# PV of two attention steps issued as one block on TensorE, in a fused attention and mixture-of-experts kernel on one core

## What is computed

```python
att = jnp.einsum('bhqd,bhkd->bhqk', q, k) / jnp.sqrt(jnp.float32(HS))
att = jnp.where(causal, att, jnp.float32(-1000000000.0))
att = jax.nn.softmax(att, axis=-1)
y = jnp.einsum('bhqk,bhkd->bhqd', att, v)
```

## Time and profile before

| | |
|---|---|
| median of three runs | 1422.44 us (1416.7 to 1422.6) |
| the profiled execution | 1421.05 us |
| its span | 1419.3 us, mean granted clock 0.94 |
| TensorE busy | 1271.5 us, 90% |
| VectorE busy | 1158.4 us, 82% |
| ScalarE busy | 777.7 us, 55% |
| GpSimd busy | 230.3 us, 16% |
| items read (line 680) | 768, 684 ns each |
| PV products (line 534) | 2560, 541 ns each |

### The profile page before, as it was taken

The page is one execution under the profiler, slowest core; times in us unless marked ns, Lnnn a source line. Parts: engine busy times, 40 slices in busy tenths (PEclk is TensorE's granted clock), DMA queues, the critical chain, the costliest instruction groups (busy, mean ns, idle before and its releaser), DMA issues. The chain is left out here.

```text
span 1419.3 us, 22655 instructions
## 1 busy us (share of the span) xinstructions
PE 1271.5 (90%) x7857; PEld 644.2 (45%) x7857; DVE 1158.4 (82%) x2780; ACT 777.7 (55%) x1098; POOL 230.3 (16%) x250
## 2 busy tenths in 40 slices
PE   8892997999999999999999999999578739999997
PEld 4550132333333333333333333332366539999997
DVE  6994997999999999899899999991276728888886
ACT  2441065666666666666666667668245435544442
POOL 1336000100100100101101100101234321111221
PEclk9995599999999999999999999999888859999999
DMA  6877496131131131121221210000545422343330
GB/s 206 255 240 167 62 155 146 31 90 32 31 91 31 33 88 32 48 74 31 61 60 32 75 46 10 23 2 16 165 142 181 154 92 93 101 142 117 96 105 21
DMA packets 120272, 126.91 MB, mean 89 GB/s; under 512 B 16604, under 2 KB 102751, under 8 KB 120160
## 3 DMA queue, kind: packets, MB, share of 16 engines
q1 hardware_dynamic: 116576, 117.01, 29.7%
q0 software_dynamic: 3584, 8.47, 1.7%
HBM read 83.02 MB, written 48.38 MB: 93 GB/s over the span
## 5 line engine op out<-in xcount | busy, mean ns | idle before, releaser
L625 ACT ACTIVATE probs<-scores 128x1024 f32<-128x1024 f32 (+3 forms) x640 | 539.0, 894 | 327.9 <-PE scores L518 327.0
L680 DVE TENSOR_REDUCE part_max<-ring 128x1 f32<-128x512 f32 x768 | 478.4, 684 | 24.0 <-PE ring L548 22.4
L548 PE MATMUL ring<-k_stack,q_stack 96*128 96x512 bf16 (+3 forms) x1280 | 407.1, 363 | 41.1 <-DMA k_stack<-pieces_d 26.2
L518 PE MATMUL scores<-q_stack,k_stack 99*128 99x512 bf16 (+3 forms) x1280 | 339.8, 350 | 9.9 <-DMA q_stack<-max_rows 7.6
L534 PE MATMUL out_p<-probs,v_s 128*32 128x512 f32 (+3 forms) x2560 | 300.2, 541 | 0.5 <-POOL probs L730 0.3
L548 PEld LDWEIGHTS ring<-k_stack,q_stack 96*128 96x128 bf16 x1280 | 114.9, 97 | 347.9 <-DVE part_max L680 148.7
L674 DVE CUSTOM_DVE_ANT_0 scratch<-ring,mask_s 128x384 f32<-128x384 f32 (+2 forms) x384 | 195.0, 551 | 18.0 <-issue 17.1
L730 POOL TENSOR_SCALAR_AFFINE_SELECT probs<-probs 128x512 f32<-128x512 f32 x128 | 81.6, 637 | 781.8 <-ACT probs L625 781.8
L518 PEld LDWEIGHTS scores<-q_stack,k_stack 99*128 99x128 bf16 x1280 | 113.0, 98 | 182.7 <-issue 64.3
L1394 PE MATMUL psY<-w_hi,h_hi 128*128 128x256 f32 x320 | 90.9, 284 | 0.0
L534 PEld LDWEIGHTS out_p<-probs,v_s 128*32 128x32 f32 x2560 | 50.6, 108 | 87.3 <-issue 56.2
(11 more groups left out here) (113 smaller groups left out, 1349.9 us busy)
## 6 DMA issues: line engine op xcount, KB each, us to landing
w_whole<-w SPq DMA_DIRECT2D x16, 1024.0 KB, 7.5
q_stack<-pieces_d SPq DMA_DIRECT2D x192, 64.0 KB, 3.0
k_stack<-pieces_d SPq DMA_DIRECT2D x192, 64.0 KB, 3.1
v_d<-vt SPq DMA_DIRECT2D x8, 1024.0 KB, 4.6
v_s<-v_d SPq DMA_DIRECT2D x8, 1024.0 KB, 6.0
o_d<-o_s SPq DMA_DIRECT2D x32, 256.0 KB, 2.2
p_o<-o_d SPq DMA_DIRECT2D x8, 1024.0 KB, 6.0
slots_d<-no_row SPq DMA_DIRECT2D x1, 5200.0 KB, 28.3
```

Source lines behind the costliest of these rows:

```text
L518: last = nc.tensor.matmul(scores[p][:, hh, off:CHUNK], k_stack[i][0:KROWS, kb // TPC, j, kb % TPC * P:(kb % TPC + 1) * P], q_stack[i][0:KR ...
L548: last = nc.tensor.matmul(slot[:, h * w:(h + 1) * w], q_stack[i][0:SROWS, qt // TPC, j + h, qt % TPC * P:(qt % TPC + 1) * P], k_stack[i][0 ...
L625: nc.scalar.activation(probs[n % NPROB][:, 2 * p:2 * p + 2, off:CHUNK], scores[p][:, :, off:CHUNK], ACT.Exp, scale=SCALE).then_inc(exp_don ...
L680: nc.vector.tensor_reduce(part_max[:, qt, j, t:t + 1], ring[m % 3][:, 0:w], axis=AX.X, op=ALU.max).then_inc(ring_read, 1)
```

## The change

PV is left out of the even steps, and an odd step n issues the PV of the steps n - 3 and n - 2 one directly after the other (`pv_pair`), in the place where it issued that of n - 2. Everything else on TensorE keeps its order, the items too. On ScalarE the copy of `out_p` after a chunk's last PV moves from behind the second exponential of an odd step to between the two exponentials of the even step after it. VectorE's, GpSimd's and SyncE's instructions stay as they are.

```diff
-assert NSTEP % NPROB == 0
+PAIR = 2
+assert NSTEP % NPROB == 0 and all(last % PAIR == PAIR - 1 for last in LAST)
...
                 items(u, i, uses, second, third, ahead)
                 if behind:
-                    pv_step(*behind)
+                    pv_pair(*behind)
                 items(u, i, uses, third, stop, ahead)
+
+            def pv_pair(u, i, n):
+
+                for m in range(n - PAIR + 1, n + 1):
+                    pv_step(u, i, m)
 
             def unit(u, i, uses, ahead):
 
                 for n in range(LAG, NSTEP):
                     if n == LAG:
                         pe.wait_ge(v_loaded[i], 16 * uses[0])
-                    step(u, i, uses, n, ahead, (u, i, n - LAG))
-                for n in range(NSTEP - LAG, NSTEP):
-                    if ahead:
-                        step(u + 1, 1 - i, uses[1:], n + LAG - NSTEP, ahead, (u, i, n))
-                    else:
-                        pv_step(u, i, n)
+                    step(u, i, uses, n, ahead, (u, i, n - LAG) if n % PAIR else None)
+                if ahead:
+                    for n in range(LAG):
+                        step(u + 1, 1 - i, uses[1:], n, ahead, (u, i, NSTEP + n - LAG) if n % PAIR else None)
+                else:
+                    pv_pair(u, i, NSTEP - 1)
...
             def exp_step(u, n):
                 off = STEPS[n][2]
                 for p in range(2):
+                    if p == 1:
+                        if n == LAG and u:
+                            copy_o(u - 1, 0)
+                        for c in ORDER:
+                            if n - LAG - 1 == LAST[c]:
+                                copy_o(u, c)
                     act.wait_ge(scores_ready[p], NSTEP * u + n + 1)
...
-            def unit(u, follows):
+            for u in range(UNITS):
                 for n in range(NSTEP):
                     exp_step(u, n)
-                    if n == LAG - 1 and follows:
-                        copy_o(u - 1, 0)
-                    for c in ORDER:
-                        if n - LAG == LAST[c]:
-                            copy_o(u, c)
-
-            unit(0, False)
-            for u in range(1, UNITS):
-                unit(u, True)
             copy_o(UNITS - 1, 0)
```

## The result

The changed kernel takes 1488.25 us (median of four runs, 1487.0 to 1489.9) against 1422.41 us for the kernel before (now four runs too), a ratio of 1.0464 with a 95% interval of 1.0442 to 1.0486: slower by 4.6%. The forecast was 1488.

A forecast was written before the change was run, and what follows sets the result against it. VectorE plus a small PV hole was taken to bound five-item steps, TensorE four-item ones. Seven units at 8.9 us (62), last unit 9.5, less 4 absorbed: +67 us on 1421, 1488 us, range 1455 to 1518.

The forecast's parts named there:

- The bound: Full-width attention steps with five items: VectorE bounds them, plus a 0.09 us hole from the PV block; 3.08 us per step.
- The hole: VectorE's standstill across a full-width joined PV block: 0.99 us in place of 0.09; eight cycles per unit lose 4.1 us.
- the 29 us faster: Rival: TensorE is the bound and saved switches shorten 160 pairs by about 0.2 us each, giving 1392 us; chance 0.05.
- The starts of chunks: Five cycles per unit at the start of a chunk or its maxima: the longer joined block adds 4.0 us.
- The narrow cycles: Seven cycles per unit with narrow blocks or four to five items: together +0.7 us, between -1 and +2.
- The 0.5 us for the copy in step 38: The moved copy of out_p lies between two exponentials of 256 columns and delays the next scores: +0.5 us.
- The last unit: Second-half scores wait for exponentials, some six cycles at about +1.0 us; with the first half's +3.5, +9.5 us.
- Unit 0: A TensorE wait for the DMA of a maximum's rows absorbs the 4 us lost before it.
- A sign that failed: In the list of waits, VectorE's idle before ring reads was to rise from 20.5 us to well over 100.
- The other signs: Unit 111 to 112 us, blocks 1.90, cycles 6.4 and 7.0, VectorE busy 95, TensorE waiting in its own row, clock 1.00.
- The rivals: Other outcomes: faster 0.05, cancelled out or not done 0.05, falling clock 0.04; those outside the range hold 0.14.
- The clock's: Rival: TensorE's pauses in the attention drop its clock to 1.2 GHz in one cycle of six, 117 us more, 1605; chance 0.04.

The follow-up runs named there:

- ring2_single: The kernel before with a ring of two PSUM banks in place of three: 1541.98 us, ratio 1.0847.
- ring4_single: The kernel before with a ring of four banks, one head's scores left out of the result: 1400.39 us, ratio 0.9843 to the kernel before.
- half_single: The kernel before with VectorE's plain ring reads cut from 512 to 256 columns: 1395.46 us, ratio 0.9822 to the kernel before.
- The ring experiments: The kernel before and the changed kernel, each rebuilt with two and four ring banks: 1541.98 and 1400.39 us, against 1606.45 and 1440.55.
- copy_back: The changed kernel with the copy of out_p put back behind the second exponential of an odd step: 1482.84 us, 1.0437 to the kernel before.
- half_joined: The changed kernel with VectorE's plain ring reads cut from 512 to 256 columns: 1436.11 us, ratio 1.0106 to the kernel before.
- ring2_joined: The changed kernel with a ring of two banks in place of three: 1606.45 us, ratio 1.1302 to the kernel before.
- split: The changed kernel with one item put between an odd step's two PV steps, where one is left: 1503.8 us, 1.0580 to the kernel before.
- ring4_joined: The changed kernel with a ring of four banks, one head's scores left out: 1440.55 us, ratio 1.0127 to the kernel before.

## Why the prediction was right

**The bound.** That the five-item step hangs on VectorE, with a hole of 0.09 us, was worked out from distances between rows, while the busy shares of TensorE and VectorE looked alike. `ring2_single` bears it out: the same sum with one read less gave its five-item step to 0.01 us. So do `ring4_single` and `half_single`: with the hole closed or the reads shorter, a full-width step of five items takes 3.05 us in both in place of 3.09. That is a small gain, and not where most of their 21 and 26 us come from, twice and more what was expected. In a mid-run unit of `ring4_single` (99.9 us for 102.8) most lies in steps with narrow scores or masked reads: step 12 falls from 3.09 to 2.84, since its five reads bound a step whose work on TensorE is less. In `half_single` 13 of the 26 us lie ahead of the first PV (173.7 us in place of 186.6), where the first maxima are made. So VectorE bounded the kernel before in more places than I had counted.

**The hole.** 0.99 us was forecast for a joined block and 0.94 measured, with a cycle of ten items at 6.83 us for 6.98 and of nine at 6.32 to 6.56 for 6.38 (6.45 where one item follows the block, 0.1 more, as it said). The block was 1.86 us, not 1.90: the second PV step pays neither start nor end, so it lies at the lower bound. The Trainium skill (TensorEngine Tiling (Array Packing), Key Properties) says that a change of the tiling mode, and not just of the tile, drains TensorE. The trace agrees: joining saved 0.14 us of two blocks' time and 0.10 of an entry. But the program did not get the 29 us faster that this alone was to give (160 pairs at 0.2 us would be 32), since TensorE's saved time fell into waits.

**The starts of chunks.** +4.0 us per unit as forecast. The working took the longer block to be paid in full there. The ring experiments show this for two of the five cycles (0.86 us with any number of banks); the other three cost less with two or four banks, so for them it is not shown.

**The narrow cycles** came out at +0.4 for +0.7. The 0.5 us for the copy in step 38 was right: by `copy_back` it is 0.46. Without the copy the joined order gains there, 2.99 us for 3.16, and the seven cycles together -0.1, where the working had left +0.2.

**The last unit** lost 10.6 us for 9.5. Its full-width joined cycles were right (5.03 for 5.07), but the same cycles before take 4.17 and not 3.94, so that they and four like them lose 0.86 each and not 1.0. On the other side I had put the two cycles whose even step is narrow at about nothing, and they lose 0.78 each: there, too, the scores of 128 columns wait for exponentials, now of 256.

**Unit 0.** I let 4 us be absorbed by the wait for a DMA. That wait shrank only from 7.6 to 5.8 us, so the absorption was 2. The mid-run units came out at +8.4 in place of +8.9 each (3 us less in all), the last unit and the clock at 1 and 2 us more, and the stages after the attention, which I had left alone, took 1.3 us less. These errors cancelled: forecast +67 us, measured +67.5 in the span. That the sum is right to a microsecond is luck to about the size of these terms, some 3 us.

**A sign that failed.** VectorE's idle time before plain reads of the ring was to rise from 20.5 us to well over 100. The list shows 57.9 (59 waits of about 1 us). VectorE's whole idle time from 250 to 970 us does come to 115, but only some nine waits in a unit stand before plain reads; the rest lies around the masked reads and at the starts of chunks. So this sign was put on the wrong row. The other signs came as written, the clock apart: unit, block, cycles, VectorE's busy time, and TensorE's waits for these reads in its own row (18.5 us, 0.6 before).

**The rivals.** The clock's was there, but small: 2 us where it would have been 117, since TensorE fell to 1.2 GHz in two places and not in every sixth cycle. The forecast's "1.00 throughout" was wrong by that much. The Trainium skill (TensorE: Matmul & The Clock Gate, A second HAM failure mode: psum-queue depth-cycling) tells of a kernel in which brief pauses between groups, as it goes round PSUM banks, make the clock swing. The traces agree in so far as in the joined order with two banks the clock fell twelve times. They don't say that the pauses do it: `ring2_single`, which waits too (TensorE busy 91% from 260 to 980 us, 93% in the changed kernel), has no such place. Why it fell where it did stays open; nothing was run for it.

## What to carry to other kernels

Where two engines hand each other buffers, look at the longest stretch in which the producer does something else, not at busy shares: the consumer lives through it only if (buffers + 1) times its time per buffer covers the stretch and the way through the ring (here 0.74 + 0.32 + 0.42 us, one read included). Joining work to save switches lengthens just that stretch. By this count it would take more buffers to earn the saving; with one bank more the joined order was still 40 us slower than the single one, and no run here has it faster. And a reordering is paid again wherever a third engine used the removed work as cover, as ScalarE did with PV between two steps' scores.

## What the runs showed of the hardware

In the attention the granted clock fell to 1.2 GHz for a few microseconds at a time in the profiled executions of six kernels, all with joined blocks or with two PV steps close together, and in none with the single order. In the changed kernel, `half_joined` and `ring2_joined` TensorE's longest pause in the ten microseconds before such a stretch was 0.4 to 0.9 us; in `split`, `copy_back` and `ring4_joined` it was 1.2 to 1.8. A stretch of 3.4 us cost 1.1 to 1.6 us.

Two PV steps in a row took 1.86 us where two apart took 2.00, with the second set of four 32-column products following at the pace of passes within one step. A fourth item in a row waited 0.25 us for its bank with three banks even when VectorE's read was cut to half its columns: the way to VectorE and back, 0.42 us before the read and some hundredths after it, is then what counts. Splitting an exponential over two banks (0.92 us from start to start) into two over one bank each (0.48 us) cost ScalarE little: 74.8 us busy per unit in place of 69.1.
